# The first loads on two queues, and the first projections batch by batch, in a two-layer decoder kernel

## What is computed

```
x = ln(x + attn0(x));  x = ln(x + quantized_expert(x, f, ctx));  x = ln(x + ternary_ffn(x))
x = ln(x + attn1(x));  x = ln(x + xattn(x, ctx));                x = ln(x + moe_top2(x))

attn0: q = x Wq' + bq (16 heads of 16), k = x Wk' + bk, v = x Wv' + bv (4 heads of 16)
       q, k = rope(rms_norm(q)) * q_gain, rope(rms_norm(k))
       out = softmax(causal(q k' / 4)) v;  return out Wo' + bo
ternary_ffn: w is replaced by round(w / mean|w|) clipped to -1, 0, 1, for w1 and w2
```

## Time and profile before

| | us |
|---|---|
| three runs | 508.55, 509.94, 512.79 |
| median of them | 509.94 |
| the profiled execution, its own time | 507.93 |
| its span, first to last instruction | 506.2 |
| busy in the span: PE, DVE, ACT, POOL | 402.6, 343.6, 242.7, 107.5 |

### The profile page before, as it was taken

The page is one execution under the profiler, slowest core; times in us unless marked ns, Lnnn a source line. Parts: engine busy times, 40 slices in busy tenths (PEclk is TensorE's granted clock), DMA queues, the critical chain, the costliest instruction groups (busy, mean ns, idle before and its releaser), DMA issues.

```text
span 506.2 us, 8074 instructions
## 1 busy us (share of the span) xinstructions
PE 402.6 (80%) x3090; PEld 312.7 (62%) x3090; DVE 343.6 (68%) x782; ACT 242.7 (48%) x432; POOL 107.5 (21%) x111
## 2 busy tenths in 40 slices
PE   2906578998885554599998688999987899999993
PEld 2506545676644443378766565667766689888883
DVE  0489698777677749576648888656946485666545
ACT  1558714655433863367557714446535324422230
POOL 4400005449311630042183000000101710000001
PEclk9957598999897886579999999999989999999998
DMA  6900020000000000000000006970000000000101
GB/s 203 296 5 1 1 70 5 3 4 1 2 2 0 0 2 0 0 1 0 3 0 1 1 1 87 116 149 3 2 0 1 0 2 1 0 1 0 43 1 42
DMA packets 13126, 13.33 MB, mean 26 GB/s; under 512 B 2904, under 2 KB 12448, under 8 KB 12832
## 3 DMA queue, kind: packets, MB, share of 16 engines
q1 hardware_dynamic: 12224, 12.54, 11.3%
q10 hardware_dynamic: 864, 0.27, 0.3%
HBM read 11.56 MB, written 1.05 MB: 25 GB/s over the span
## 4 chain that ended last, share of the span: by engine, by line
PE 60%; DVE 21%; ACT 11%; issue 3%; POOL 1%; DMA 1%; SPq 0%; DVEq 0%; POOLq 0%; ACTq 0%
PE PS L2146 12%; PE PS L2163 6%; ACT arena L750 5%; PE PS L1761 4%; PE PS L1845 4%; DVE mx L1263 3%; PE PS L2073 3%; PE PS L383 3%; PE PS L1886 3%; PE PS L2086 3%; PE PS L1813 3%; PE PS L1739 2%; PE PS L1855 2%; PE PS L1642 2%; DVE arena L1152 2%
## 5 line engine op out<-in xcount | busy, mean ns | idle before, releaser
L869 ACT ACTIVATE PT<-PS 128x512 f32<-128x512 f32 x96 | 53.5, 594 | 36.3 <-PE PS L1813 36.2
L2146 PE MATMUL PS<-arena_r 128*128 128x512 f32 x264 | 64.6, 393 | 2.2 <-ACT xT L750 2.2
L666 POOL TENSOR_SCALAR va<-mv 128x4 f32<-128x4 f32 x12 | 5.3, 443 | 273.3 <-DVE mv L1099 273.3
L2146 PEld LDWEIGHTS PS<-arena_r 128*128 128x128 f32 x264 | 48.0, 188 | 11.9 <-issue 2.7
L750 ACT ACTIVATE arena<-PS 96x1024 bf16<-96x1024 bf16 (+4 forms) x59 | 44.5, 810 | 22.5 <-PE PS L1739 11.3
L1739 PE MATMUL PS<-ident,arena 128*96 128x128 bf16 x416 | 30.7, 241 | 28.9 <-DVE arena L1142 27.5
L1739 PEld LDWEIGHTS PS<-ident,arena 128*96 128x96 bf16 x416 | 28.7, 141 | 32.7 <-DVE arena L1142 29.2
L1761 PE MATMUL PS<-masks,ident 128*128 128x512 bf16 x112 | 43.2, 386 | 4.7 <-DVE mx L1263 2.4
L1263 DVE TENSOR_REDUCE mx<-PS 128x4 f32<-128x1024 f32 x32 | 39.0, 1218 | 1.2 <-PE PS L1793 0.2
L2163 PEld LDWEIGHTS PS<-arena_r 128*128 128x128 f32 x264 | 34.4, 191 | 2.5 <-DVE arena_r L1564 0.9
L2163 PE MATMUL PS<-arena_r 128*128 128x256 f32 x264 | 35.1, 283 | 0.7 <-DVE arena_r L1564 0.7
(11 more groups left out here) (218 smaller groups left out, 904.7 us busy)
## 6 DMA issues: line engine op xcount, KB each, us to landing
arena<-in_L_ffn_w SPq DMA_DIRECT2D x16, 176.0 KB, 10.2
arena<-in_L_ffn_w SPq DMA_DIRECT2D x2, 1024.0 KB, 10.2
arena<-in_L_ffn_w SPq DMA_DIRECT2D x2, 704.0 KB, 7.5
arena<-in_fside_BxS2xS SPq DMA_DIRECT2D x1, 1024.0 KB, 12.7
out<-x SPq DMA_DIRECT2D x4, 256.0 KB, 2.5
x<-in_x SPq DMA_DIRECT2D x1, 768.0 KB, 8.6
arena<-in_L_attn_Wq SPq DMA_DIRECT2D x2, 256.0 KB, 4.5
arena<-in_L_attn_Wo SPq DMA_DIRECT2D x2, 256.0 KB, 6.4
```

The costliest lines, as they stand in the source:

```text
L869: nc.scalar.activation(PT[:, n % 2, 512 * j:512 * (j + 1)], bank(3 + j), ACT.Exp, scale=NEG_SCALE)\
L2146: last = mm(bank(2 * (n % 2) + gu), wp[c][:, gu, c_ * P:(c_ + 1) * P], xp[5][:, c, blk * 512:(blk + 1) * 512], start=(step == 0 and c == 0 ...
```

## The change

It does these things:

- Wk and Wv are issued first on ScalarE's queue. On SyncE's queue Wq stands ahead of x of batch 0, and the rest of x is split into batch 1 and batches 2 and 3, with a semaphore more (`x1_loaded`).
- TensorE turns x of batch 0, waits for the weight copies, projects tiles 0 and 1, turns x of batches 1 and 2, projects tiles 2 and 3, turns x of batch 3 and projects tiles 4 to 7. Its waits for `const` and `tables` stand behind the projections, ahead of the stack transposes.
- ScalarE copies xT of batch 3 behind `squares(1)`, not ahead of `squares(0)`.
- `abs_sums` stands between the stack copies of batch 0 and of batch 1, not behind `squares(1)`. `absw` lies at offset 15360 and not at 1024, since Qh is being written by then.
- Semaphores that a layer doesn't use are no longer made.

```diff
-        absw = carve(1024, [P, 2048], BF16)
+        absw = carve(15360, [P, 2048], BF16)
...
+            sp.dma_start(wq0n[:, 0:2, :], t["L0_attn_Wq"].rearrange("(r p) d -> p r d", p=P)).then_inc(w["l0"], 16)
             sp.dma_start(x[:, 0:2, :], xv[:, 0:2, :]).then_inc(x_loaded, 16)
-            sp.dma_start(wq0n[:, 0:2, :], t["L0_attn_Wq"].rearrange("(r p) d -> p r d", p=P)).then_inc(w["l0"], 16)
-            sp.dma_start(wq0n[0:64, 2, :], t["L0_attn_Wk"]).then_inc(w["l0"], 16)
-            sp.dma_start(wq0n[64:128, 2, :], t["L0_attn_Wv"]).then_inc(w["l0"], 16)
-            sp.dma_start(x[:, 2:TT, :], xv[:, 2:TT, :]).then_inc(x_rest_loaded, 16)
+            sp.dma_start(x[:, 2:4, :], xv[:, 2:4, :]).then_inc(x1_loaded, 16)
+            sp.dma_start(x[:, 4:TT, :], xv[:, 4:TT, :]).then_inc(x_rest_loaded, 16)
...
             w = w_loaded
+            act.dma_start(wq0n[0:64, 2, :], t["L0_attn_Wk"]).then_inc(w["l0"], 16)
+            act.dma_start(wq0n[64:128, 2, :], t["L0_attn_Wv"]).then_inc(w["l0"], 16)
             act.dma_start(bqkv[:, 0:D], t["L0_attn_bq"].partition_broadcast(P)).then_inc(qkv_bias_loaded, 16)
...
                 if L == 0:
                     squares(0)
                     squares(1)
-
-                    abs_sums()
+                    evac_xT(0, 3, 4)
+
                     for b in (0, 2):
...
                         evac_stacks(L, b)
+                        if b == 0:
+                            abs_sums()
                         evac_stacks(L, b + 1)
...
-            evac_xT(0)
+            evac_xT(0, 0, 3)
             attn_front(0)
...
-                        pe.wait_ge(x_rest_loaded if b else x_loaded, 16)
+                        pe.wait_ge((x_loaded, x1_loaded, x_rest_loaded, x_rest_loaded)[b], 16)
...
                 if L == 0:
-                    for tt in range(TT):
+                    transpose_x(0, 0, 1)
+                    copied_out(pe, NG0 - 1)
+                    project_tile(0)
+                    project_tile(1)
+                    transpose_x(0, 1, 3)
+                    project_tile(2)
+                    project_tile(3)
+                    transpose_x(0, 3, 4)
+                    for tt in range(4, TT):
                         project_tile(tt)
+                    pe.wait_ge(w_loaded["const"], LOADS["const"])
+                    pe.wait_ge(w_loaded["tables"], LOADS["tables"])
                     stack_transposes(0, 0)
                     stack_transposes(0, 1)
...
             pe_groups(pe, 0, NG0 - 1)
-            transpose_x(0)
-            copied_out(pe, NG0 - 1)
-            pe.wait_ge(w_loaded["const"], LOADS["const"])
-            pe.wait_ge(w_loaded["tables"], LOADS["tables"])
             project(0)
```

More of the change, by code:

```diff
@@ L250, in post_ln_decoder_two_layers @@
         x_loaded = sem("x_batch0_loaded")
+        x1_loaded = sem("x_batch1_loaded")
         x_rest_loaded = sem("x_rest_loaded")
@@ L285, in post_ln_decoder_two_layers @@
         A = [{k: sem(f"l{L}_{k}") for k in
-              ("proj", "proj_read", "lat", "lat_ready", "v_ready", "hi", "rem", "mid", "lo", "squared", "stk_tr",
-               "sq", "ev_act", "ev_dve", "smax", "mx", "mst", "mtr", "mT", "mrow", "sT", "pT", "av", "os", "ot2", "on",
-               "otr", "OT")} for L in range(2)]
+              ("proj", "v_ready", "hi", "rem", "mid", "lo", "stk_tr",
+               "ev_act", "ev_dve", "smax", "mx", "mst", "mtr", "mT", "mrow", "sT", "pT", "av", "os", "ot2", "on",
+               "otr", "OT") + (("proj_read", "squared", "sq") if L == 0 else ("lat", "lat_ready"))} for L in range(2)]
         Q = {k: sem(f"q_{k}") for k in
@@ L650, in residual_bias @@
                     if stage == 0:
-                        pool.wait_ge(x_rest_loaded if b else x_loaded, 16)
+                        pool.wait_ge((x_loaded, x1_loaded, x_rest_loaded, x_rest_loaded)[b], 16)
                         if b == 0:
```

## The result

| | before | after |
|---|---|---|
| median of 18 runs, us | 509.45 | 513.86 |
| lowest and highest | 507.82, 514.33 | 510.75, 517.55 |
| ratio after to before (95% interval) | | 1.0066 (1.0039 to 1.0092) |
| span of the profiled execution | 506.2 | 512.1 |

The account below looks back on a forecast made before the run. Bounds before the second stack transposes: TensorE's wait for Wv until 9.85, VectorE's chain, then ScalarE's evacuations and high parts. Front gain -3.2 plus sums' loss +4.1 gave +0.9 on 509.8, so 510.7 us; range 506.2 to 513.9.

Parts of the forecast that it names:

- Part 3, the sums: ScalarE's absolute sums between stack evacuations: a loss of 4.1 us in full (3.9 to 4.2), VectorE waiting about 5 us.
- Part 2, the front's gain: TensorE's new order up to tile 3's projection: done at 16.6 instead of 19.8, gaining 3.2 us (1.9 to 4.5).
- Part 1, the loads: Start of the DMA queues: Wq and small weights there at about 5.8, x of batch 0 at 7.6 instead of 9.85.
- All behind it start 3.2 us earlier: VectorE's chain behind the projections: the front's whole gain passes on, sums of squares at 18.05 for 21.25.
- The bytes ahead: Landing of x of batch 0: 968 KB through the shared DMA engines by 8.1, taking 0.5 us from the gain.
- R1: Rival at the loads: x of batch 0 lands only at 9.85, front gains 1.0, total +3.1, 512.9 us; chance 0.17.
- R3: Rival at the loads: Wk and Wv no sooner than 9.85, front gains 0 to 0.8, 513.1 to 513.9 us; chance 0.06.
- R2: Rival at the stack evacuations: the sums fit into ScalarE's waits and cost nothing, -3.2, 506.6 us; chance 0.12.
- R4: Rival in later stages: the granted clock falls differently after the shift, either way by 2 us; chance 0.10.
- Its own signs: First matmul near 6, tile 3 at 15.3 to 17.9, sums of squares near 18, last stack transposes at 57 to 58.
- The forecast's own range: Whole kernel time: 509.4 to 512.0 us, from a front gain of 1.9 to 4.5 us with the loss of 4.1.
- The whole range: Whole kernel time with the rivals: 506.2 to 513.9 us, from R2 with a partly better front to R3.

Follow-up runs that it names:

- e1: The changed kernel with the two absolute sums back ahead of the high parts, absw left at its new place; ratio to the kernel before 0.9954.
- e2: The kernel before with only the absolute sums moved between the stack copies of batches 0 and 1, and absw's new offset; ratio to before 1.0067.
- e5: The kernel of e1 with VectorE instead of ScalarE making the first two copies (turned weight group 0, xT of batch 0); ratio to before 0.9971.
- e7_order: The kernel of e1, but TensorE turns batches 0 and 1, projects tiles 0 to 3, then turns the rest; VectorE's reads await biases alone; ratio to before 0.9942.
- e8_all: The kernel of e7_order plus VectorE's copies (both weight groups, xT of batches 0 and 1) and nine unread products on TensorE; ratio to before 0.9943.
- e10_adds_later: The kernel of e7_order with GpSimd's eight additions of x and bo made to wait for VectorE's first row maximum; ratio to before 0.992.
- e12_best_no_products: Against e1: VectorE copies weights and batch 0's xT, batch 1 turned behind tiles 0, 1, the rest behind tile 3, biases-only reads, later additions, no products; ratio to before 0.9951.

## Why the prediction was right, and where it was not

- **Part 3, the sums: right.** 4.1 us were expected on ScalarE's path, in full. The high parts came 3.85 later with a front 0.11 earlier at the first stack copy (40.26 for 40.37): 3.96. VectorE's wait was 4.58 for about 5. e1 and e2 show that it is this edit alone.
- **Part 2, the front's gain: mis-sized, 0.25 us at tile 3 for 3.2**, and outside its own bounds (1.9 to 4.5, and 1.0 with x at its latest). Term by term from 16.6 to 19.55: the first projection at 9.70 for 9.3 (+0.4); tiles 0 and 1 both at 1.2 GHz, 5.46 for 3.86 (+1.6), since one of them was put at 2.4 GHz, and a tile at 1.2 GHz took 2.73 and not 2.57; between tile 1 and tile 2 the x transposes and ScalarE's copy of batch 1 took 1.54 for 0.85, since tile 2 waits for a copy that starts only when its four transposes end, a wait that the sum did not have (+0.7); tiles 2 and 3 2.86 for 2.57 (+0.3).
- **Part 1, the loads: wrong on both sides.** The weights landed by 4.7 (5.8), x of batch 0 at 5.2 (7.6; issued at 1.71, 3.5 us), and TensorE came to it at 6.15. That should have given 1.4 us more. It did not, because the part counted ScalarE's two more issues only for what they load. They also stand ahead of its own table load and its first copies. The two themselves took 0.55 and 0.61 us, but the last two of the eight took 0.95 and 2.18, and the table load started at 7.28 for 3.71 before and ended at 8.56. The prediction had ScalarE free whenever TensorE was done; e5 shows what that was worth.
- **What stands behind the front.** "All behind it start 3.2 us earlier" would have failed even with that gain: e7_order starts the sums of squares 2.80 us before the kernel before, and the second stacks 1.44. 1.2 us of the difference are instructions held by GpSimd's additions (7.73 for 6.54 us from the sums of squares to the rotation), which the prediction does not name.
- **The bytes ahead.** The prediction's estimate of 8.1 for x of batch 0 was worked out from the rule of the Trainium skill that all queues end on the same DMA engines (DMA: Bandwidth & Descriptors, Issuing engines are not separate DMA queues). x was there at 5.2. That speaks against counting all bytes ahead; the rule itself is not tested by it.
- **The rivals.** R1 and R3 gave times near the measured one (512.9; 513.1 to 513.9), and "a front that gains next to nothing" is what happened, but by neither's mechanism: x was early and so was TensorE, and the signs of both (a first matmul after 8, a gap of over 2 us ahead of the x transposes) are absent. What ate the head start was the clock, taken as one tile of two, and ScalarE's queue, taken as free. R2 is refuted by e2. R4 moved the profiled execution by 2.9 us behind the first row maximum (5.9 for 3.0), more than its 2.
- **Its own signs.** Right were the sums between the stack copies and VectorE's wait. The first matmul was even earlier (4.84 for 6), but tile 3 (19.55 for 15.3 to 17.9), the sums of squares (21.00 for 18) and the last stack transposes (60.74 for 57 to 58) were not where they should have been.
- The sum with the measured terms: -0.11 + 3.96 = +3.85 at the high parts; the means of 18 runs say +3.4.
- **The range held by luck.** The forecast's own range (509.4 to 512.0) did not hold 513.86. The whole range did, by 0.04 us, since it reached to a front without gain, which it had for another reason (R3).

## What to carry over

Before work is moved "out of the way" on an engine, look at which stretch of that engine is the path and which is idle: 4 us of ScalarE's work cost nothing at 21 us and their full length at 45. DMA issues on an engine that also computes are work of that engine, ahead of whatever it does next. A head start on a path of TensorE that stood idle counted at the low clock first, and unread products ahead of it bought that back (5.46 to 2.82 us). And what a head start is worth is read at the end of the path: here other engines' work, which did not move with it, took up to 1.8 us back.

## What was not expected of the hardware

- A DMA issue is not of a fixed cost: on ScalarE's queue 0.40 to 0.61 us each up to about 3.6 us, and then 0.45 to 2.37 us for the next ones, different from trace to trace. Whether the time or the number of DMAs then queued decides, these traces don't tell, and the cause stays open.
- The page's clock row reads 1.00 at the start of the span, while the durations (847 and 421 ns for 486 and 272) show 1.2 GHz until 13.1 at least in the kernel before, and until 14.3 at least in the changed one.
- VectorE's instruction of 0.20 us takes 0.77 beside GpSimd's additions of 0.73, and in e8_all and e5_vector_copies three in a row are held.
- x of batch 0, third on SyncE's queue behind the same two loads, landed between 5.2 and 5.8 us in nine traces, and at 7.4 and 7.7 in e10_adds_later and e12_best_no_products. Nothing that was edited explains the difference.
